# The first 54 jobs of the row maxima moved from the attention stage into the projections

## What is computed

```python
x = x + _layernorm(_L0_attn_ref(_layernorm(x), wq, bq, wk, bk, wv, bv, wo, bo))
x = x + _layernorm(_L0_ffn_ref(_layernorm(x), Wr, br, W1, b1, W2, b2))
# attention: q, k, v = x @ w + b; scores * SCALE, causal mask, softmax, @ v, then @ wo + bo
# ffn: two of 8 experts per batch, chosen by the first row; gelu between two 256 x 256 layers
```

## Time and profile before

| | |
|---|---|
| median of 3 runs | 2087.66 us |
| the profiled execution's own time | 2087.79 us |
| its span | 2086.1 us |
| TensorE busy | 1992.6 us (96%) |
| VectorE busy | 1829.1 us (88%) |
| ScalarE busy | 1348.1 us (65%) |
| GpSimd busy | 250.1 us (12%) |
| mean granted TensorE clock | 0.974 |

### The profile page before, as it was taken

One profiled execution on the slowest core, in us unless ns is written; L12 is line 12 of the kernel. 1 busy time (PEld: TensorE's weight loads), 2 busy tenths in 40 slices (PEclk: granted clock), 3 DMA queues, 4 the chain that ended last, 5 costly groups with the idle time before them and its releaser, 6 DMA issues.

```text
span 2086.1 us, 39561 instructions
## 1 busy us (share of the span) xinstructions
PE 1992.6 (96%) x15696; PEld 874.1 (42%) x15696; DVE 1829.1 (88%) x3611; ACT 1348.1 (65%) x1637; POOL 250.1 (12%) x349
## 2 busy tenths in 40 slices
PE   6998999999999999999999999999999996999997
PEld 3665333333333333333333333333333324667654
DVE  6877898999999999999999999999999926899873
ACT  3666346777777777777777777777777781333332
POOL 3000000100101110010111001010100104322000
PEclk9999588999999999999999999999999998999999
DMA  3799220413315042321505143140514024553320
GB/s 117 239 267 259 72 42 11 83 43 59 66 29 89 8 88 43 59 67 28 89 8 88 33 68 62 33 89 8 88 34 68 12 93 106 138 139 107 88 66 30
DMA packets 143755, 162.53 MB, mean 78 GB/s; under 512 B 52178, under 2 KB 117970, under 8 KB 143570
## 3 DMA queue, kind: packets, MB, share of 16 engines
q1 hardware_dynamic: 136658, 147.39, 31.2%
q0 software_dynamic: 6912, 12.61, 2.8%
HBM read 99.90 MB, written 59.77 MB: 77 GB/s over the span
## 4 chain that ended last, share of the span: by engine, by line
PE 77%; DVE 14%; ACT 4%; DMA 2%; issue 2%; SPq 1%; POOL 0%; ACTq 0%; DVEq 0%; POOLq 0%
PE b_psO L1000 25%; PE b_psS L983 25%; PE b_ring L964 14%; DVE b_pmax L886 3%; PE a_psQK L562 3%; PE c_psH L1363 3%; PE c_psO L1376 2%; PE a_psV L572 2%; PE b_ring L962 1%; DMA a_x<-in_L_attn_x 1%; DVE c_attn L105 1%; DVE c_ln_x_stats L81 1%; DVE c_ln_f_stats L81 1%; ACT b_prob L924 1%; PE c_psA L1333 1%
## 5 line engine op out<-in xcount | busy, mean ns | idle before, releaser
L886 DVE TENSOR_REDUCE b_pmax<-b_ring 128x1 f32<-128x512 f32 (+3 forms) x2336 | 1365.9, 646 | 80.2 <-PE b_ring L964 65.1
L924 ACT ACTIVATE b_prob<-b_psS 128x1024 f32<-128x1024 f32 (+3 forms) x1280 | 1085.0, 895 | 384.5 <-PE b_psS L983 380.6
L983 PE MATMUL b_psS<-g_qT,g_kT 33*128 33x512 bf16 (+7 forms) x5120 | 849.0, 351 | 7.8 <-ACT b_prob L924 5.6
L964 PE MATMUL b_ring<-g_kT,g_qT 64*128 64x512 bf16 (+3 forms) x2560 | 750.2, 354 | 2.0 <-DVE b_pmax L886 1.7
L1000 PE MATMUL b_psO<-b_prob,g_v 128*32 128x512 f32 (+3 forms) x5120 | 601.0, 545 | 0.4 <-POOL b_prob L876 0.4
L983 PEld LDWEIGHTS b_psS<-g_qT,g_kT 33*128 33x128 bf16 (+1 forms) x5120 | 301.7, 95 | 457.4 <-ACT b_prob L924 333.7
L876 POOL TENSOR_SCALAR_AFFINE_SELECT b_prob<-b_prob 128x512 f32<-128x512 f32 x256 | 163.1, 637 | 1540.4 <-ACT b_prob L924 1540.1
L964 PEld LDWEIGHTS b_ring<-g_kT,g_qT 64*128 64x128 bf16 x2560 | 232.3, 95 | 254.0 <-DVE b_pmax L886 177.9
L962 PE MATMUL b_ring<-later,query_of 64*128 64x128 bf16 x1024 | 202.5, 222 | 8.5 <-DVE b_pmax L886 6.4
L1000 PEld LDWEIGHTS b_psO<-b_prob,g_v 128*32 128x32 f32 x5120 | 103.8, 108 | 168.0 <-issue 132.1
L1363 PE MATMUL c_psH<-c_yT,c_w1e 128*128 128x512 f32 x256 | 121.0, 618 | 21.0 <-ACT c_hT L1295 21.0
(11 more groups left out here) (96 smaller groups left out, 994.7 us busy)
## 6 DMA issues: line engine op xcount, KB each, us to landing
qk_parts<-a_parts SPq DMA_DIRECT2D x64, 384.0 KB, 4.5
g_qT<-qk_parts SPq DMA_DIRECT2D x192, 128.0 KB, 4.1
g_kT<-qk_parts SPq DMA_DIRECT2D x192, 128.0 KB, 5.5
out_sums<-b_outT SPq DMA_DIRECT2D x64, 256.0 KB, 2.7
v_ones<-a_v SPq DMA_DIRECT2D x16, 544.0 KB, 5.8
g_v<-v_ones SPq DMA_DIRECT2D x32, 272.0 KB, 6.0
a_x<-in_L_attn_x SPq DMA_DIRECT2D x16, 512.0 KB, 5.7
c_x<-in_L_attn_x SPq DMA_DIRECT2D x16, 512.0 KB, 7.3
```

The costliest lines, as they stand in the source:

```text
L886: nc.vector.tensor_reduce(pmax[:, c % 2].rearrange("p (h t) n -> p h t n", t=TT)[:, heads[0]:heads[-1] + 1:2, qt, pc], ring[:, r % BANKS, ...
L924: nc.scalar.activation(prob[:, j % PBUF, 2 * s:2 * s + 2, off:CH], psS[:, 2 * s:2 * s + 2, off:CH], ACT.Exp).then_inc(exp_done, 1)
L964: ins_ = nc.tensor.matmul(to, qT[own, g, h // 2, 0, t * P:(t + 1) * P], kT[own, g, h // 2, 0, pc * CH:pc * CH + w], start=pc < c, stop=Tru ...
L983: ins_ = nc.tensor.matmul(psS[:, 2 * s + p, off:CH], kT[own, g, s, ab, kt * P:(kt + 1) * P], qT[own, g, s, ab, c * CH + off:(c + 1) * CH], ...
```

## The change

1. **Leads.** The first 54 entries of the list of jobs (52 jobs and 2 turns) leave `ORDERS` and are done in stage A, in chunks 7 to 15, six a chunk, two at each of three places: after the second of the four query and key outputs, after the turn of the next chunk, and after the values. They use a ring of two PSUM banks. To make room, `psQK` shrinks from four banks to two, and TensorE waits for ScalarE to have emptied the output two before.
2. **Subtractions.** `rest = full - high part` moves from VectorE to GpSimd (one instruction of 128 x 2048). The middle cast and the low subtraction of a chunk now stand in the next chunk: on ScalarE between its second and third output, on VectorE between the first and second lead. `full` has two buffers, `rest` one. Those of chunk 15 are done in stage B, at key steps 1 and 3, and its stores at step 6.
3. **Values.** ScalarE copies the values out of PSUM (one instruction of 128 x 1024, after the high cast) instead of VectorE adding the bias. The bias goes through `wo`: in stage C `bo` becomes `bo + bv @ wo`, with two VectorE products, two matmuls against ones and one addition before the first step.
4. **Loads.** `x` has three buffers and is loaded one chunk earlier. The first group's queries and keys for the maxima are loaded in halves: 16 half parts in chunks 3 and 4 (eight each), 16 in chunks 5 to 8 (four each), then the 10 other parts, two a chunk, in chunks 9 to 13. The values of a chunk are stored before its parts.
5. **A new `ORDERS`** for what is left. It begins

The core of the diff (the strings of `ORDERS`, the moved helpers and the semaphores' names are left out):

```diff
+LEAD_FROM = 7
+LEAD_TIMES = 3
+LEAD = 2 * LEAD_TIMES * (B * NC - LEAD_FROM)
+FIRST_HALF = 3
+SECOND_HALF = 5
+def leads(n, k):
+    at = 2 * ((n - LEAD_FROM) * LEAD_TIMES + k)
+    return [] if at < 0 else list(enumerate(FIRST_JOBS))[at:at + 2]
...
+    def wait_bank(self, pe, r):
+        before = r - 2 if r < LEAD else r - BANKS if r > LEAD else -1
+        if before >= 0:
+            pe.wait_ge(self.ring_free, before + 1)
...
 # stage A, GpSimd
+            for n in range(N):
+                pool.wait_ge(hi_done, n + 1)
+                if n > 0:
+                    pool.wait_ge(low_done, n)
+                nc.gpsimd.tensor_tensor(rest[:, :], full[n % 2], parts[:, n % 2, :, 0], ALU.subtract
+                                        ).then_inc(rest_done, 1)
 # stage A, VectorE
+            for n in range(N):
+                chain = variance(n + 2) if n + 2 < N else None
+                lead(n, 0)
+                if n > 0:
+                    low(v, n - 1)
+                lead(n, 1)
+                if chain:
+                    normalise(chain, n + 2)
+                lead(n, 2)
 # stage A, ScalarE
+            for n in range(N):
+                evict(n, 0)
+                evict(n, 1)
+                if n > 0:
+                    middle(act, n - 1)
+                evict(n, 2)
+                evict(n, 3)
+                if n + 2 < N:
+                    root(n + 2)
+                if n + 1 < N:
+                    copy_xT(n + 1)
+                if n >= 2:
+                    act.wait_ge(stored[n % 2], n // 2 * 16 * STORES)
+                act.wait_ge(evicted, (n + 1) * 2 * KD)
+                nc.scalar.copy(parts[:, n % 2, :, 0], full[n % 2]).then_inc(hi_done, 1)
+                copy_v(n)
 # stage A, TensorE
+            for n in range(N):
+                pe.wait_ge(xT_done, n + 1)
+                for i in range(2 * KD):
+                    if n * 2 * KD + i >= 2:
+                        pe.wait_ge(evicted, n * 2 * KD + i - 1)
+                    ...
+                    if i == 1:
+                        lead(n, 0)
+                if n + 1 < N:
+                    turn(n + 1)
+                lead(n, 1)
+                if n > 0:
+                    pe.wait_ge(v_copied, n)
+                ...
+                lead(n, 2)
 # stage B
-            act.wait_ge(stores.last_v, 1)
-            r = 0
+            r = LEAD
 # stage C, VectorE
+            for k in range(KD):
+                ins_ = nc.vector.tensor_scalar(wob[:, k], wo[:, k], consts.bv[:, k:k + 1], None, ALU.mult)
+            ins_.then_inc(bias_scaled, 1)
+            v.wait_ge(bias_summed, 1)
+            nc.vector.tensor_tensor(consts.bo[:, :], psO[:, 0], consts.bo[:, :], ALU.add).then_inc(o_read, 1)
```

More of the change, by code:

```diff
@@ L290 @@
[L290 to L306, removed]
@@ new lines, with first_jobs, leads_of @@
+LEAD_FROM = 7
[3 more added lines that the diff above has]
+SECOND_HALF = 5
+def first_jobs():
+    jobs = max_jobs()
+    return [job if job[0] == "turn" else (*job, not any(other[:4] == job[:4] for other in jobs[r + 1:]))
+            for r, job in enumerate(jobs[:LEAD])]
+FIRST_JOBS = first_jobs()
+def leads(n, k):
+    at = 2 * ((n - LEAD_FROM) * LEAD_TIMES + k)
+    return [] if at < 0 else list(enumerate(FIRST_JOBS))[at:at + 2]
+def leads_of(n):
+    return [job for k in range(LEAD_TIMES) for job in leads(n, k)]
@@ L735, in read_orders @@
             left[job[1:4]] = left.get(job[1:4], 0) + 1
-    order, at, taken, turned, valued = [], [0, 0], [0, 0], 0, 0
+    for job in jobs[:LEAD]:
+        if job[0] == "max":
+            left[job[1:4]] -= 1
+    order, at, valued = [], [0, 0], 0
+    taken = [sum(n < LEAD for n in units_of[p]) for p in range(2)]
+    turned = sum(n < LEAD for n in turns)
     for sign in "".join(ORDERS):
@@ L768, in stage_b, with stage_a @@
+def stage_a(nc, block, sems, ins, qk_scr, v_scr, consts, groups, chunks, stores, maxima):
     with ExitStack() as ctx:
@@ new lines, in stage_a @@
+        xT = chunks.cc[:, 0:2]
+        full = [tile[:, i:i + 2].rearrange("p b k n -> p (b k) n") for tile, i in ((chunks.cc, 2), (chunks.inv, 0))]
+        rest = chunks.inv[:, 2:4].rearrange("p b k n -> p (b k) n")
+        v_sb, parts, stored = stores.v_sb, stores.parts, stores.stored
+        ln = LayerNorm(nc, sb, "a_ln")
+        psQK = pb("a_psQK", [P, 2, CH], F32)
+        psT = pb("a_psT", [P, KD, CH], F32)
+        ring = pb("a_ring", [P, 2, CH], F32)
+        psV = pb("a_psV", [P, TT, D], F32)
@@ new lines, in stage_a, with scalar, vector, sync @@
+        class Rest:
+            @staticmethod
+            def scalar(act):
+                middle(act, N - 1)
+            @staticmethod
+            def vector(v):
+                low(v, N - 1)
+            @staticmethod
+            def sync(sp):
+                store(sp, N - 1)
+        return Rest
+def stage_b(nc, block, sems, consts, groups, chunks, stores, maxima, rest_of_a):
+    with ExitStack() as ctx:
+        def sb(name, shape, dt):
+            return ctx.enter_context(nc.sbuf_tensor(name, shape, dt))
+        def pb(name, shape, dt):
+            return ctx.enter_context(nc.psum_tensor(name, shape, dt))
+        def sem(name):
+            return sems.enter_context(nc.semaphore(name))
+        qT, kT, vS = groups.qT, groups.kT, groups.vS
@@ L852, in _ @@
                 elif what == "turn":
-                    place_max(*which, r)
+                    maxima.place(sp, r, *which)
                     r += 1
```

785 lines of the change are left out of this document (397 added, 388 removed).

## The result

The changed kernel takes 2066.14 us, the median of 4 runs (2065.89 to 2067.85), beside 2089.8 for the one before: a ratio of 0.989 (95% interval 0.987 to 0.992). The profiled execution took 2067.85, with a span of 2066.1, 20.0 less than the old span.

The account below looks back on a forecast made before the run. TensorE was taken to bound stage A and the body of stage B, VectorE's reductions to pace its opening. Leads +13.5, late banks +4.5, SyncE's queue +2 and stage B -35 gave -15: 2072.8 us, range 2054 to 2092.

Parts of the forecast that it names:

- What bounds the kernel: TensorE bounds stage A at 11.19 us a chunk; VectorE's lone reductions pace the 154.35 us opening of stage B.
- The leads on TensorE: Stage A: the led jobs add 13.5 us to TensorE, plus 4.5 us of waiting for late banks.
- VectorE in a lead chunk: Stage A: VectorE loses 3.6 us and gains 3.5, so 9.2 us in a chunk of 12.7 to 13.
- GpSimd's subtraction: Stage A: the 128 x 2048 subtraction on GpSimd lies between 2.34 and 4.68 us; the upper bound was taken.
- The loop: Stage A: ScalarE and GpSimd's round of casts, subtraction and evictions takes 11.5 us against TensorE's 11.19; slack covers it, cost 0.
- SyncE's queue: Stage A: sixteen added load issues hold the queue in chunks 3 and 4; between 0 and 5 us, 2 taken.
- The opening: First 38 steps of stage B: VectorE work falls to 102 us, old idle 19.7 kept; 122 us, a gain of 32.6.
- Stage C: The bias products, matmuls and addition before the first projection, under 2 us, hide behind a GpSimd wait: cost 0.
- 1: Slower rival: GpSimd holds VectorE in stage A, lead chunks last 15.6 us and the clock falls; 2105 us, chance 0.14.
- 2: No-change rival: TensorE starves in stage B's opening and the clock falls again, gain 17 us; 2091 us, chance 0.14.
- 3: Rival: the ScalarE and GpSimd loop, 12.9 us with collisions, paces every chunk of stage A; 2081 us, chance 0.13.
- 4: Rival: the new order is better in stage B's body as well, by up to 10 us; 2063 us, chance 0.05.

Follow-up runs that it names:

- no_leads_block: Changed kernel with no leads; all 54 jobs stand as a block ahead of the new order up to step 90, then the old one: 2077.2 us.
- joined_order: Changed kernel with the new order up to the middle of step 90 and the old order from there: 2061.7 us, ratio 0.987.
- no_leads: Changed kernel with no jobs led in stage A and the old order of stage B: 2086.8 us, ratio 0.999 to the kernel before.
- leads_old_order: Changed kernel with all 54 leads, but stage B runs the old order without its first 54 entries: 2075.6 us, ratio 0.993 to the kernel before.
- subtract_twice: Changed kernel with GpSimd doing its subtraction twice in every chunk: 2115.8 us in one run.

## Why the prediction was right

The forecast was 2072.8 with a range of 2054 to 2092, for 15 us less than the profiled execution of before; 20.0 were measured on the spans, and 2066.14 lies within the forecast's own range too. The mechanism is the forecast's: VectorE's work leaves the opening for less than it cost there. That the number came so near is in part luck, since its terms miss in both directions: stage A +20 forecast and +12.5 measured, the opening -32.6 and -38.8, the rest of stage B -2 and +5.6. Two of the signs named for a right forecast did not come, both on the good side: stage A ends at 216.16, not at 220 to 226, and step 38 at 331.4, not at 340 to 348. The body's 5.6 is just under the 6 that was to mean wrong. By its steps:


- **What bounds the kernel** held: stage A is TensorE's, the opening VectorE's. no_leads_block against joined_order shows it: 28 us of VectorE's work taken away, 28.8 us of time to step 16.
- **The leads on TensorE**: 13.5 forecast and 14.0 measured, but not of the same parts. The jobs themselves took 9.2, less than the sum had from the lengths of single records, and the products behind each lead took 0.2 longer, 4.8 in all, which no term had. The 4.5 us for late banks were not there: in the chunk shown the reductions end at 167.48, 171.30 and 175.99, and the next leads begin at 169.72, 174.55 and 178.53; from 102 to 216 the view of waits has none of TensorE for a reduction.
- **VectorE in a lead chunk**: 9.2 forecast without collisions. Measured 8.6 on average over nine chunks (77.41), of which the last two have no layernorm to prepare; in the six whole ones from 114.67 to 191.79 it is 56.65, 9.4 each.
- **GpSimd's subtraction**: 4.68 taken, 4.07 to 4.12 measured. The 4.50 of the Trainium skill's page "GPSIMD Engine Reference" is nearer than my bound, and still above; the measurement decides. The loop was forecast at 11.5, just over TensorE's chunk, and measured at 10.1. The two evictions took 1.17 in it, since they are partly done before the middle cast ends, and the handovers to and from GpSimd 0.07 and 0.02.
- **SyncE's queue**: 2 us taken, 0 measured; the chunks after the heavy loads are 11.2 long. Stage A even lost 1.8 us (168.7 to 166.9 in no_leads) of waits that the kernel before had, which no term counted. With a start 0.3 later, 14.0 - 1.8 + 0.3 gives the 12.5.
- **The opening**: forecast 122, measured 115.2. VectorE's busy time, 102 forecast, is 103.33. The mis-sized term is its idle time, 19.7 kept and 11.9 measured. leads_old_order shows where that is decided: with the same leads and the old order it is 22.2. I had costed the new order at nothing, within 6 either way; it took 9.2 off the opening between the two profiles (124.4 to 115.2; 11.7 by estimate, 13.3 less 1.6, if the clock behind step 16 were the same) and added 4 to 5 in the body. The leads alone, with the old order, would have given 2075.6: in the range; the other 9.5 us of the median are the order's, for a term that I had put at nothing. In the bounds of the opening, the 5 us of first-step latency and the 8 added to 99/0.77 had no row behind them.
- **Stage C**: 0 forecast, 0.7 measured between the profiled runs; the same stretch varied by 10 between the others (359.2 to 369.1), so nothing can be told.
- **The rivals.** 1 did not happen: VectorE is held, but off the path, and in the lead chunks hardly at all. subtract_twice shows what it would look like. 2: the clock did fall twice, for 23.9 us in all instead of 71.7; the second fall cost 5 us, as one of 13.7 us did before (65.7 against 60.2), so it doesn't enter the difference. 3: the loop has 1.1 us of room. 4: the order was worse in the body, not better, by 4.1 to 4.8 us from step 80 to 618.

## What to carry over

When a stage begins with work for one engine alone, look in the stage ahead of it for an engine that idles in every round: the same jobs cost 0.26 us each beside a TensorE-bound stage and 0.53 where they stood alone. Count the interruption as well as the jobs: a third of the 0.26 fell on the products behind them. Moving them pays fully only if what remains is spread anew; with the old order cut down, the last 24 of 54 jobs gave little more than they cost. And a new order should be compared piece by piece: here the best kernel takes its opening from one and its body from the other.

## What was not expected of the hardware

A cast of 1.90 us and a 4.1 us GpSimd operation hand over in 0.02 to 0.07 us, and GpSimd's two-input operation on 128 x 2048 float32 costs 4.07, less than twice the 2.34 of 128 x 1024, though the second input is bfloat16 in the one and float32 in the other. Two bfloat16 jobs set between the float32 products make the products behind them 0.2 us longer (3.63 against 3.43 for eight records), a cost for which no row of the kernel before stood. And low clock has no one price: its first 7.5 us at the seam, where VectorE was busy 9.71 of 10 us, changed nothing when they were taken away, while behind step 16 a fall of 6.8 us cost 2.2 to 2.6 and one of 13.7 cost 5.1 to 5.5, in either order.
